# Loads issued ahead in the weight quantization, and a norm stage moved ahead of a quantization stage, in a transformer layer on eight cores

## What is computed

```python
x = x + _layernorm(attn(_layernorm(x), W_qkv, W_o))
x = x + _layernorm(ffn(_layernorm(x), w1, b1, w2, b2, gamma, beta))

def act_quant(x):
    scale = 127.0 / clip(max(abs(x), axis=-1), EPS)
    return clip(round(x * scale), -128, 127), scale
def weight_quant(w):
    scale = 1.0 / clip(mean(abs(w)), EPS)
    return clip(round(w * scale), -1, 1), scale
def qlinear(x, w, b):
    xq, sx = act_quant(x)
    wq, sw = weight_quant(w)
    return einsum('bsd,hd->bsh', xq, wq) / (sx * sw) + b
# ffn: h = layernorm(x)*gamma+beta; qlinear(gelu(qlinear(h, w1, b1)), w2, b2)
```

## Time and profile before

| | us |
|---|---|
| median of 2 timed runs | 4159.47 (4153.91 to 4165.03) |
| the profiled execution | 4132.81 |
| its span, slowest of 8 cores | 4131.2 (the others from 4106.4) |
| TensorE busy | 2123.8 (51%) |
| VectorE busy | 1525.3 (37%) |
| ScalarE busy | 719.7 (17%) |
| POOL busy | 132.2 (3%) |

### The profile page before, as it was taken

One profiled execution on the slowest core, in us unless ns is written; L12 is line 12 of the kernel. 1 busy time (PEld: TensorE's weight loads), 2 busy tenths in 40 slices (PEclk: granted clock), 3 DMA queues, 4 the chain that ended last, 5 costly groups with the idle time before them and its releaser, 6 DMA issues.

```text
span 4131.2 us, 33823 instructions; the slowest of 8 cores (4106.4 to 4131.2 us)
## 1 busy us (share of the span) xinstructions
PE 2123.8 (51%) x10640; PEld 1046.1 (25%) x10640; DVE 1525.3 (37%) x2492; ACT 719.7 (17%) x1185; POOL 132.2 (3%) x203
## 2 busy tenths in 40 slices
PE   0011101227657656367475664665665637656565
PEld 0011101114422222144222222342222224422222
DVE  0311142123445443233454431444544323354442
ACT  0010001111212112121122111222222112222121
POOL 0111100000000000000000000000000000000000
PEclk9999995556668878666687776666888866678777
DMA  9533353431121111311211113112111131131111
GB/s 203 150 54 57 57 182 74 67 63 26 31 94 29 36 28 29 119 26 29 99 24 36 36 32 111 31 29 92 31 28 36 33 113 28 32 99 31 25 29 44
DMA packets 333137, 245.50 MB, mean 59 GB/s; under 512 B 304272, under 2 KB 304288, under 8 KB 328864
## 3 DMA queue, kind: packets, MB, share of 16 engines
q0 software_dynamic: 97440, 184.58, 16.1%
q1 hardware_dynamic: 235520, 58.74, 7.6%
HBM read 159.41 MB, written 33.55 MB: 47 GB/s over the span
## 4 chain that ended last, share of the span: by engine, by line
PE 39%; DMA 23%; DVE 18%; ACT 9%; issue 8%; DVEq 1%; another core or an unknown queue 0%; SPq 0%; ACTq 0%; POOLq 0%; POOL 0%; PEldq 0%; PEld 0%
PE pb L959 13%; PE pb L877 13%; DMA af<-w 9%; DMA abf<-abf 5%; PE pb L481 5%; DMA af<-x 4%; PE pb L488 3%; DMA w2q_t<-w2qs 2%; PE pb L880 2%; PE pb L355 2%; PE pb L393 1%; DMA out<-x 1%; DVE af L326 1%; DVE af L328 1%; DMA wqkv_t<-w_qkv 1%
## 5 line engine op out<-in xcount | busy, mean ns | idle before, releaser
L877 PE MATMUL pb<-w1q_t,abf 128*128 128x512 fp8e4 x2048 | 531.8, 407 | 297.0 <-DMA abf<-abf 284.7
L959 PE MATMUL pb<-w2q_t,abf 128*128 128x512 fp8e4 x2048 | 522.3, 420 | 296.3 <-ACT s2rowr L948 263.0
L959 PEld LDWEIGHTS pb<-w2q_t,abf 128*128 128x128 bf16 x2048 | 212.4, 106 | 588.5 <-issue 401.7
L877 PEld LDWEIGHTS pb<-w1q_t,abf 128*128 128x128 bf16 x2048 | 189.1, 102 | 566.0 <-issue 406.2
L892 DVE TENSOR_REDUCE khs<-af 128x1 f32<-128x1024 f32 x128 | 156.2, 1220 | 460.2 <-ACT af L888 434.7
L481 PE MATMUL pb<-abf,wqkv_t 128*128 128x128 bf16 x2048 | 195.5, 287 | 218.0 <-DMA abf<-abf 218.0
L481 PEld LDWEIGHTS pb<-abf,wqkv_t 128*128 128x128 bf16 x2048 | 190.9, 135 | 221.9 <-issue 221.9
L326 DVE TENSOR_SCALAR af<-af,swc,mw 128x1024 f32<-128x1024 f32 (+1 forms) x48 | 47.5, 990 | 519.5 <-DMA af<-w 519.5
L355 PE MATMUL pb<-identf,af 128*128 128x128 f32 x256 | 62.1, 423 | 312.0 <-DVEq L193 312.0
L888 ACT ACTIVATE af<-pb,scal 128x512 f32<-128x512 f32 x256 | 162.1, 684 | 274.8 <-PE pb L880 269.5
L393 PE MATMUL pb<-identf,af 128*128 128x128 f32 x256 | 61.5, 420 | 234.3 <-DVEq L193 233.9
(11 more groups left out here) (162 smaller groups left out, 2694.8 us busy)
## 6 DMA issues: line engine op xcount, KB each, us to landing
af<-w POOLq DMA_DIRECT2D x16, 2048.0 KB, 9.8
wqkv_t<-qkvs POOLq DMA_DIRECT2D x3, 6144.0 KB, 20.2
af<-w POOLq DMA_DIRECT2D x32, 512.0 KB, 4.8
af<-w POOLq DMA_DIRECT2D x16, 1024.0 KB, 7.8
af<-x POOLq DMA_DIRECT2D x32, 512.0 KB, 3.9
w1q_t<-w1qs POOLq DMA_DIRECT2D x4, 4096.0 KB, 12.8
w2q_t<-w2qs POOLq DMA_DIRECT2D x4, 4096.0 KB, 22.0
out<-x POOLq DMA_DIRECT2D x32, 512.0 KB, 2.9
```

The source lines that it names most:

```text
L877: PE.matmul(Bk[bb0 + n2][:, :], lhsT=xf[:, kk, :], rhs=w1q[:, kk, hs0:hs0 + 512], start=(kk == 0), stop=False)
L959: mi = PE.matmul(Bk[4 + n2][:, :], lhsT=xq2_fm[:, kk, :], rhs=w2q[:, kk, n2 * 512:n2 * 512 + 512], start=(kk == 0), stop=False)
```

## The change

In both quantization loops the loads are issued ahead of use: six tiles ahead for w1, three for w2. After that the load of tile t+6 (or t+3) stands in POOL's queue between the store of tile t-1 and that of tile t. In the feed-forward loop the call `f_front(gg + 2)` moves from behind `f_f1(gg + 1)` to ahead of `f_q2(gg)`. What is computed stays the same.

```diff
+            ldh = {}
+            for t in range(6):
+                if t == 0:
+                    GP.wait_ge(s_dv, ms[f"prep_mean_{which}"])
+                ldh[t] = gd_dma(fsl[t % 8], wsrc_t[:, t, :])
             for t in range(32):
                 s4, s8 = t % 4, t % 8
-                if t >= 8:
-                    GP.wait_ge(s_pe, ms[f"prep_pt_{which}_{t-8}"])
-                elif t == 0:
-                    GP.wait_ge(s_dv, ms[f"prep_mean_{which}"])
-                ld = gd_dma(fsl[s8], wsrc_t[:, t, :])
-                wait_gd(V, ld)
+                wait_gd(V, ldh[t])
...
+                if t + 6 < 32:
+                    if t >= 2:
+                        GP.wait_ge(s_pe, ms[f"prep_pt_{which}_{t-2}"])
+                    ldh[t + 6] = gd_dma(fsl[(t + 6) % 8], wsrc_t[:, t + 6, :])
                 GP.wait_ge(s_ac, ms[f"prep_ev_{which}_{t}_1"])
...
+            ldh = {}
+            for ht in range(3):
+                if ht == 0:
+                    GP.wait_ge(s_dv, ms[f"prep_mean_{which}"])
+                ldh[ht] = gd_dma(fsl[ht % 4],
+                                 wsrc_t[:, ht // 2, (ht % 2) * 2048:(ht % 2) * 2048 + 2048])
...
+                if ht + 3 < 16:
+                    if ht >= 1:
+                        GP.wait_ge(s_pe, ms[f"prep_pt_{which}_{ht-1}"])
+                    nh = ht + 3
+                    ldh[nh] = gd_dma(
+                        fsl[nh % 4],
+                        wsrc_t[:, nh // 2, (nh % 2) * 2048:(nh % 2) * 2048 + 2048])
...
             if gg + 1 < G:
                 f_front_tp(gg + 1)
+            if gg + 2 < G:
+                f_front(gg + 2)
             f_q2(gg)
             if gg + 1 < G:
                 f_f1(gg + 1)
-                if gg + 2 < G:
-                    f_front(gg + 2)
             f_f2(gg)
```

More of the change, by code:

```diff
@@ L371, in prep_w @@
             tsl = [pw_t2[:, 0:16, :], pw_t2[:, 16:32, :]]
+            ldh = {}
[4 more added lines that the diff above has]
+                                 wsrc_t[:, ht // 2, (ht % 2) * 2048:(ht % 2) * 2048 + 2048])
             for ht in range(16):
                 i_, hh = ht // 2, ht % 2
[L374 to L380, removed]
+                wait_gd(V, ldh[ht])
                 quant3(f"q{which}_{ht}", fsl[ht % 4], fsl[ht % 4])
```

## The result

The changed kernel takes 3622.32 us (median of 11 runs, 3616.52 to 3678.47), the kernel before 4163.76 us beside it (10 runs): a ratio of 0.871, interval [0.8685, 0.8734]. (The 3678.47 is an execution in which the cores of one die ran slower at a lower granted clock, and the ratio leaves it out.) That is 541 us less. The direction, the order of the two weight terms and the place of the gain were right; the sizes were too cautious, most of all that of the moved f_front.

The account below looks back on a forecast made before the run. It took unoverlapped weight-tile loads and, in feed-forward, two TensorE holes (the second from ScalarE's order) as bounds; 260 + 185 + 16 = 461 off 4132.8 gave 3672 profiled, 3699 median, range 3650 to 3775 (chance 0.70).

Parts of the forecast that it names:

- So DMA: w1 preparation: with loads prefetched, the store and load pair sets the tile period, taken as 3.7 us.
- the terms 260 and 185: Weight preparation: us gained by prefetching w1 (260, ends 225 to 285) and w2 (185, ends 170 to 215).
- the slow start of f2: Feed-forward: a short hole does not spare f2 its slow first 48 matmuls, 12.21 us after 1.60 us idle.
- the first iteration: Feed-forward, gg = 0 of each segment: the moved f_front delays f_q2, a loss of 7.7 us.
- the term 16: Feed-forward: moving f_front ahead of f_q2 gains 16 us over four segments, ends 45 gained and 35 lost.
- the longer price of a switch: ScalarE table switch at 2.66 us instead of 1.28: 27 us more in all, the f_front move then losing 11.
- Rival 2: Feed-forward: the moved f_front costs more, up to 51 us more, 3750 us; chance 0.12.
- rival 3: Weight preparation: all eight cores load and store without pause, HBM slows it, 4257 us; chance 0.02.
- rival 4: Weight preparation: loads held by POOL's in-order waits for a store, only f_front's move acts, 4143 us; chance 0.03.
- The 26.7 us added at the end: Whole kernel: median of two timed runs minus profiled execution, added to turn 3672 us into 3699.
- Rival 1: Weight preparation: POOL's DMA issues and VectorE's passes exclude each other, middle price 45 us, 3744 us; chance 0.13.
- the mild case: w1 preparation: POOL and VectorE exclude each other, giving a period of 4.1 us, 13 us more in all.

Follow-up runs that it names:

- the first part alone: The changed kernel with f_front(gg+2) put back behind f_f1(gg+1), the prefetch kept; 3686.32 us, ratio 0.8862 against the kernel before.
- The repeat: The kernel before, unchanged, run and profiled once more; median of 8 runs 4165.56 us, profiled execution 4165.51 us.

## Why the prediction missed

Two kinds of term failed. In the sum for the weights, the step "So DMA" took the time of a lone store and load as the period: the terms 260 and 185 measured 270 and 196 us (466 against 445, and 478 in the run of the first part alone). In the sum for f_front, the price of the iterations was wrong, the slow start of f2 and the first iteration above all: the term 16 measured 66 us in the traces and 60 in its own run.

**Right.** The two weight terms carry the gain; their loads' wait went to 31 us (I had said under 150); s2rowr's wait is 1.6 us an iteration; the mid-f1 hole of 3 us and the table load at f_tail came as written. From the end of the ScalarE operation ahead of that table load (950.68 + 0.68) to the start of the one behind it (952.67) are 1.31 us, so the longer price of a switch that the prediction weighed beside it does not show. Rival 2 (the moved f_front costs more) went the other way, and rival 3 (memory, slower) and rival 4 (loads not early) are excluded by the first waits above.

**Wrong: "So DMA", in the prefetch of w1.** I read a lone pair's 3.93 us as the rate of pairs, and thought that it could overlap a little, to 3.7. It was a latency: loads of other tiles fill it, the DMA share goes to 1.34, and the period is VectorE's, 2.87, near the lower end (2.6) that I had written beside it. Taking one of VectorE's passes away moved w1 by 17 us, which shows that the bound is there. The term was 260 and measured 270. It came so near partly by luck: 0.83 us too much in 25 periods are 21 us, but with VectorE as the bound all 32 tiles pay the period and not 25, which took back about half. For **w2** I took 7.0 for the same reason, from the lone pair's 6.88; (425.17 - 327.03)/16 is 6.1 with start and end included, where the prediction's stretch of 110 us makes 6.9. The term was 185 and measured 196. Here I had also written that I would not go below 6.9 because of the two output buffers; with two the stretch came out below it, and four buffers changed 2 us, so this reason was wrong as well. What bounds w2 stays open.

**Wrong in size: the moved f_front.** This is the largest miss: 66 us by the table, 60 by its own run, against 16. By parts, over the four segments and against the second profile of before:

- The 16 steady iterations went from 59.5 to 53.4 us on average, 97 in all; I had 59.0 to 54.8, 67. Half a microsecond each is that I took my "before" from four iterations of one segment. In the iteration shown, the rest is f2: it took 14.6 where I took 16.4, "a little less after a shorter idle time", and it started 0.7 later than I had it.
- The first iteration of a segment lost about 3.6 us (66 less the 81 that the seven others gained, over four), where I had lost 7.7: 16 us in four.
- gg = 1 lost 2.1 against 3.8, gg = 6 lost 2.3 against 1.3.

The claim behind the f2 term, that a short hole does not spare f2 its slow start, rested on one iteration. The same trace of before had the answer two segments further on, in the same place (gg = 6), after the same idle time:

```profile
3253.66 10.52 PE L959 MATMUL pb<-w2q_t,abf 128*128 128x512 fp8e4 x48 [1.60 <-ACT s2rowr L948]
```

Over all eight cores of that trace, 21 of the 32 f2 that follow an idle time of 1.60 us took 10.5 us, and 11 took 12.2. The row that I had picked was of the rarer kind. In the change f2 runs at the 2.4 GHz level throughout, and in the experiment with f_front behind s2rowr it starts at a lower granted clock, 0.59 on average in its first 3.3 us:

```profile
1013.70:1017.00 3.30, 3.27 (x10) 1.24 (x11) 2.61 (x4) 0.36 (x1) 0.00 (x0) 0.59 0.00 0
```

What differs ahead of it is f1: in the change it is broken by the hole of 2.79 us, in the other kernel it runs through. Over the eight cores of the change, 181 of the 192 f2 behind a broken f1 had the fast start, and 3 of the 32 behind an unbroken one; in the other kernel none of the 192 of gg 1 to 6 had it. But a hole in f1 is not needed, as the 21 of before show, and in the kernel with the tail ahead of q2, without such holes, about half are fast. What decides it stays open.

**The 26.7 us added at the end.** I took it as a constant between profile and median. The repeat shows what it was: the profiled execution I had was one in which neighbouring cores loaded in turn. For the forecast the addition did no harm, since it put the sum back on the median (4163.8 - 461 would be 3703). For reading the result it matters: from the first profile the gain looks like 502, from the second 535, and the medians give 541. The gain's terms are short by 10, 11 and 50 us in the table, 2 lie ahead of w1 and between the parts, and the last 7 of the 541 lie between profile and median; the four by which the median of before moved come off. That is the 77, but for rounding.

**Rival 1, POOL against VectorE.** It exists, and its price is small. The groups of w1, first before, then after (busy, mean ns):

```profile
L328 DVE TENSOR_SCALAR af<-af,mw 128x1024 f32<-128x1024 f32 x32 | 24.1, 753 | 2.5
```

```profile
L328 DVE TENSOR_SCALAR af<-af,mw 128x1024 f32<-128x1024 f32 x32 | 31.6, 988 | 2.5
```

The VectorE pass that stands beside POOL's issue is 0.24 us longer, 7.5 us over the 32 tiles. (VectorE's passes above 0.81 us beside POOL's issues was one of the signs that the prediction named for being wrong.) In w2, where a pass is longer, both sides grow: L328 from a mean of 1286 to 1533 ns, the store issue from 1168 to 1383, the load issue from 539 to 883. One tile of w2 in the changed kernel, VectorE and POOL:

```profile
360.27 1.35 DVE L326 TENSOR_SCALAR af<-af,swc,mw 128x2048 f32<-128x2048 f32 x1 [1.06 <-DMA af<-w]
360.70 1.68 POOL L168 DMA_DIRECT2D w2qs<-abf  x1 [7.16 <-PE pb L397]
361.69 1.71 DVE L328 TENSOR_SCALAR af<-af,mw 128x2048 f32<-128x2048 f32 x1
362.37 1.16 POOL L168 DMA_DIRECT2D af<-w  x1
```

By the rule of the Trainium skill that the prediction quoted (SBUF — State Buffer, "SBUF: two separate sides") POOL is locked out until the pass ends, and the trace agrees. The store issue ends 0.76 us after L326 does, and so do all eight store issues of w2 that begin 0.2 to 0.8 us into that pass, however long they become by it (1.29 to 1.87 us, against 1.17 with no pass beside them). The load issue ends 0.12 us after the pass that it begins in, in all nine cases of w2 (1.16 us and not 0.54) and in all 25 of w1. The other way round, the L328 that begins beside the store issue takes 1.71 us and not 1.29. What the rival had wrong is the price: it laid POOL's two issues wholly behind VectorE's passes, 4.1 us in the mild case, and they overlap for the most part, 2.87. Taking the loads off POOL shortened the mean of L328 by 47 ns only, since the store issue still stands beside the same pass.

## What to carry to other kernels

A lone transfer's time in a serial loop is a latency and no rate: when a prefetch makes it one of several in flight, the next bound is the busiest engine's own work for a tile, and the sum should start from there. Read the hole that is left after a change back through its chain (here z, tail, output, transpose): moving that order was worth 200 us (3506 to 3306), three times what the change's own move was. And compare profiles whose cores stand alike: here one execution of the same kernel lay 33 us below another, as it seems by how neighbouring cores met at their weight loads, and the difference looked like a loss in a stage that the change didn't touch. Before a price is taken from one row, look at the other rows of its kind: the slow start of f2 was one of two outcomes in the very trace that the prediction read.

## What the runs showed of the hardware

- One queue with stores and larger loads in turn moved 167 GB/s with one pair in flight (w1 of before), 234 with several (w1 of the change), and 273 when VectorE had two passes for each tile and not three.
- A DMA issue of POOL that begins inside one of VectorE's tensor_scalar passes ends a fixed time after that pass: 0.12 us for the loads in 34 of 34 cases, 0.76 us for the stores of w2 in 8 of 8. The VectorE pass that follows is longer by 0.24 us on average in w1.
- w1q_t and w2q_t (4 MB each, issued 0.6 us apart) are both there 21.5 to 22.4 us after the second issue where the neighbouring core loads 18.9 us or more apart, and after 26.2 to 28.7 where it loads within 2 us.
- After the same 1.60 us idle TensorE ran 48 matmuls in 10.52 us or in 12.21, in the same kernel: 21 and 11 times in before.
